# Summing sixteen states per channel block: from turned products of 128x128 to plain products of 128x512, with a different order of the prologue and of the work between the scans

## What is computed

```python
x_and_res = x @ W_in.T
xp, res = jnp.split(x_and_res, 2, axis=-1)
xc = silu(depthwise_conv(xp, conv_w, taps=4) + conv_b)
ssm = xc @ W_x.T                       # B, C of 16 states each, and one dt
dt = softplus(dt @ W_dt.T + b_dt)
A = -exp(A_log)
def step(h, inp):                      # over the tokens
    h = exp(A * dt_t) * h + dt_t * B_t * xt
    y_t = einsum('bed,bd->be', h, C_t) + D * xt
y = silu(y + res)
return y @ W_out.T
...
x = layernorm(x + mamba(x))
x = layernorm(x + moe_top2_of_8(x))
```

## Time and profile before

| | us |
|---|---|
| time, median of 3 runs | 1610.7 (1607.85 to 1612.19) |
| time of the profiled execution | 1612.57 |
| its span, first to last instruction | 1611.0 |
| first scan of block 0 | 61.5 |
| end of the last scan of block 7 | 995.7 |

### The profile page before, as it was taken

How to read it: one execution, slowest core, us unless ns; L and a number is a source line. 1 busy time by engine, 2 the same in 40 slices (tenths; PEclk the granted TensorE clock), 3 DMA queues, 4 the chain that set the end, 5 groups by cost and what they waited for, 6 DMA issues and landing times. The chain is left out here.

```text
span 1611.0 us, 29240 instructions
## 1 busy us (share of the span) xinstructions
PE 1336.9 (83%) x8770; PEld 1118.7 (69%) x8771; DVE 1157.4 (72%) x2036; ACT 1041.1 (65%) x1438; POOL 1059.9 (66%) x989
## 2 busy tenths in 40 slices
PE   3598898898798898798887796639999999999970
PEld 1367577576577576576577685439999999999970
DVE  2678888888888888888888687436666666666646
ACT  3798996996996996996996874413333333333334
POOL 0288878778877978877978888344444444444436
PEclk8699899999999899999899798659999999999995
DMA  2032132222222222222212223441343631511108
GB/s 98 14 99 80 63 105 76 76 80 89 92 77 89 85 84 89 92 78 88 89 67 85 90 85 122 131 129 53 107 133 117 199 121 39 160 39 40 33 26 308
DMA packets 85677, 150.12 MB, mean 93 GB/s; under 512 B 11408, under 2 KB 34576, under 8 KB 85584
## 3 DMA queue, kind: packets, MB, share of 16 engines
q1 hardware_dynamic: 70480, 116.91, 22.7%
q0 software_dynamic: 9888, 27.29, 5.1%
q10 hardware_dynamic: 5216, 4.74, 0.9%
HBM read 104.45 MB, written 44.45 MB: 92 GB/s over the span
## 5 line engine op out<-in xcount | busy, mean ns | idle before, releaser
L1019 POOL TENSOR_TENSOR arena<-arena 128x1024 f32<-128x1024 f32 x256 | 611.2, 2394 | 73.0 <-DVE arena L796 61.9
L397 PEld LDWEIGHTS d_ps<-ident,arena 128*128 128x128 f32 x2048 | 257.4, 150 | 203.0 <-DVE arena L796 101.5
L397 PE MATMUL d_ps<-ident,arena 128*128 128x128 f32 x2048 | 337.7, 291 | 73.0 <-DVE arena L796 67.5
L618 ACT ACTIVATE arena<-u_tok,b_tok 128x512 f32<-128x512 f32 x512 | 327.3, 713 | 74.4 <-PE d_ps L397 72.8
L796 DVE TENSOR_TENSOR_SCAN arena<-arena,carry,d_ps 128x512 f32<-128x512 f32 x256 | 320.6, 1271 | 74.2 <-PE d_ps L397 72.9
L796 DVE TENSOR_TENSOR_SCAN arena<-arena,d_ps 128x512 f32<-128x512 f32 x256 | 305.1, 1211 | 79.4 <-PE d_ps L397 67.6
L410 PE MATMUL y_ps<-ident,arena 128*128 128x128 f32 x2048 | 311.0, 282 | 40.6 <-POOL arena L1019 40.6
L410 PEld LDWEIGHTS y_ps<-ident,arena 128*128 128x128 f32 x2048 | 248.7, 147 | 47.3 <-POOL arena L1019 47.3
L1306 ACT ACTIVATE h_t<-ht_ps 128x512 f32<-128x512 f32 x142 | 84.5, 595 | 289.8 <-PE ht_ps L1361 289.8
L629 ACT ACTIVATE arena<-dt,neg_a 128x2048 f32<-128x2048 f32 x128 | 255.4, 1995 | 1.9 <-DVE arena L796 1.3
L1371 PEld LDWEIGHTS y_ps<-arena,h_parts 128*128 128x128 f32 x1704 | 214.4, 192 | 8.8 <-issue 4.0
(11 more groups left out here) (170 smaller groups left out, 1681.9 us busy)
## 6 DMA issues: line engine op xcount, KB each, us to landing
arena<-c_rows SPq DMA_DIRECT2D x128, 256.0 KB, 3.4
weight_parts<-arena SPq DMA_DIRECT2D x80, 256.0 KB, 3.8
arena<-weight_parts SPq DMA_DIRECT2D x20, 1024.0 KB, 5.3
arena<-in_pieces SPq DMA_DIRECT2D x80, 128.0 KB, 3.6
xg<-expert_rows POOLq DMA_DIRECT2D x71, 130.0 KB, 2.4
arena<-expert_out SPq DMA_DIRECT2D x16, 512.0 KB, 10.4
arena<-in_pieces SPq DMA_DIRECT2D x12, 512.0 KB, 7.2
x_t<-in_x_t SPq DMA_DIRECT2D x8, 512.0 KB, 5.5
```

What stands on the lines that cost most here:

```text
L397: last = nc.tensor.matmul(d_ps[:, c % 2, j * P:(j + 1) * P], ub[:, g % U_RING, j, c * P:(c + 1) * P], t.ident[:], start=True, stop=True, i ...
L618: nc.scalar.activation(ub[:, g % U_RING, j, :], u_tok[:, j, :], ACT.Identity, scale=b_tok[:, b % 2, j, n:n + 1]).then_inc(scaled, 1)
L1019: nc.gpsimd.tensor_tensor(h[:, g % H_RING, lo:hi, :], h[:, g % H_RING, lo:hi, :], c_row[:, g % C_RING:g % C_RING + 1, :].broadcast_to([P, ...
```

## The change

- `sum_states` keeps channels on the partitions: per step four matmuls with the identity as weights and 128x512 of states streaming, no transposes. `y_ps` now holds [channel, group, token].
- So `turn_y` and `yt_out` fall away; the gated output `ys` goes straight into the output projection. The silu of the sums is two instructions of 128x4x256. The gate takes `w_in` as weights and `x_t` as stream; the skip is 4 matmuls of 128x512 in place of 16 of 128x128.
- `ys` and the inputs `u` share one buffer, as `y_u` did before; `tmp` is gone.
- `D_RING` is 4 and decays are made three steps ahead, scaled inputs still two.
- The output projection, gates, ranks, skips, residuals, softplus sum, inputs and the router's steps stand at other quarters. `onehot` is one instruction in place of eight. Each row store of the router has a step of its own.
- Pieces per block fall from 10 to 8: the last expert's 16 pieces are split in the prologue, in the tiles of h (`first_part` on ACT, `first_rest` on POOL, loads and stores on SP); the first scan waits for their stores.
- The prologue has its own order on ACT: a second copy of the spread dt (`z2`) lets DVE make the linear part (`first_sizes`), the first scaled inputs are read from PSUM, and the decays of steps 0 to 2 are made before the loop. `w_in` comes in two loads, `x_t` on ACT's queue.
- In i = 8 the own weights are rounded at steps 3 to 10 in place of 6 to 13.

```diff
-D_RING = 3
+D_RING = 4
+DECAY_LEAD = 3
...
                 def sum_states(b, k):
-                    n, q = divmod(k, 4)
-                    g, half = STATE * b + n, q // 2
-                    pe.wait_ge(hc_done, 2 * g + half + 1)
+                    n, c = divmod(k, 4)
+                    g = STATE * b + n
+                    pe.wait_ge(hc_done, 2 * g + c // 2 + 1)
                     if k == 0 and b > 0:
-                        pe.wait_ge(ys_done, b)
-                    for j in (2 * (q % 2), 2 * (q % 2) + 1):
-                        for c in (2 * half, 2 * half + 1):
-                            last = nc.tensor.matmul(y_ps[:, j, c * P:(c + 1) * P],
-                                                    h[:, g % H_RING, c, j * P:(j + 1) * P], t.ident[:],
-                                                    start=(n == 0 and c == 0), stop=(n == STATE - 1 and c == EC - 1),
-                                                    is_transpose=True)
-                    if q == 3:
+                        pe.wait_ge(ys_done, 2 * b)
+                    last = nc.tensor.matmul(y_ps[:, c, :], t.ident[:], h[:, g % H_RING, c, :],
+                                            start=(n == 0), stop=(n == STATE - 1))
+                    if c == 3:
                         last.then_inc(sum_done, 1)
...
-        PIECE_STEPS = (0, 1, 3, 4, 6, 8, 9, 10, 11, 12)
-        PARTED = (EXPERTS - W_RING) * PIECES
+        PIECE_STEPS = (0, 1, 3, 4, 6, 8, 10, 12)
+        PARTED = (EXPERTS - W_RING - 1) * PIECES
...
                     act.wait_ge(sum_done, STATE * (r + 1))
-                    nc.scalar.activation(y_u[:], y_ps[:], ACT.Silu).then_inc(ys_done, 1)
+                    if r >= 1:
+                        wait_filled(act, "out1", r - 1)
+                    for lo in (0, T // 2):
+                        nc.scalar.activation(ys[:, :, lo:lo + T // 2], y_ps[:, :, lo:lo + T // 2], ACT.Silu)\
+                            .then_inc(ys_done, 1)
...
+                if i == -1:
+                    silu()
+                    act.wait_ge(t.rest_loaded, 16 * REST_LOADS)
+                    first_part(3)
+                    ssm_out()
+                    for c in range(EC):
+                        z_parts(c)
+                    soft_tail()
+                    nc.scalar.activation(t.neg_a[:], t.neg_a[:], ACT.Exp).then_inc(exp_done, 1)
+                    decays(0)
+                    xp_out(0)
+                    xp_out(1)
+                    wait_freed(act, "btok", 0)
+                    for j in range(TT):
+                        first_scale(j)
+                    for j in range(TT):
+                        ut_out(j)
+                    for j in range(TT):
+                        wait_freed(act, f"ut{j}", 0)
+                    scale(1)
+                    decays(1)
+                    decays(2)
+                    xp_out(2)
+                    xp_out(3)
+                    return
...
-                        if n == 7:
+                        if n == 8:
                             soft_tail()
...
                     if 0 <= g + LEAD < STEPS:
                         scale(g + LEAD)
-                        decays(g + LEAD)
+                    if 0 <= g + DECAY_LEAD < STEPS:
+                        decays(g + DECAY_LEAD)
...
                         if back:
-                            if at == (9, 1):
+                            if at == (7, 0):
                                 residual(0)
-                            if at == (11, 1):
+                            if at == (10, 0):
                                 residual(1)
```

More of the change, by code:

```diff
@@ L82, in _ @@
         def _(act):
+            for dst, src in early:
+                act.dma_start(dst, src).then_inc(t.first_loaded, 16)
             for dst, src in taps:
@@ L556, in between @@
+                        if 0 <= m < 8 and n < 7:
+                            out_projection(0, m, m + 1)
                     if front and at == (5, 0):
                         spread_z()
+                        if f == 0:
+                            spread_z2()
+                    if place and at == (7, 0):
+                        ranks()
+                    if front and at == (8, 1):
+                        turn_b()
                     if scans:
-                        gates = ((4, 2), (4, 3), (5, 1), (5, 2), (5, 3), (6, 0), (6, 2), (6, 3))
+                        gates = ((4, 0), (4, 3), (5, 2), (6, 1), (6, 3), (7, 1), (7, 2), (7, 3))
@@ L619, in scale, with first_scale @@
                                          scale=b_tok[:, b % 2, j, n:n + 1]).then_inc(scaled, 1)
+            def first_scale(j):
+                wait_filled(act, f"ut{j}", 0)
+                nc.scalar.activation(ub[:, 0, j, :], bank(f"ut{j}", 0), ACT.Identity,
+                                     scale=b_tok[:, 0, j, 0:1]).then_inc(scaled, 1)
             def decays(g):
@@ L753, in step @@
                         turned_out(1)
-                    if back and n == 3:
-                        yt_out(0)
-                    if back and n == 4:
-                        yt_out(1)
+                    if place and n == 4:
+                        router_exp()
                     if front and n in (5, 6):
@@ L760, in step @@
                         z_parts(2 * n - 9)
-                    if back and n in (5, 6):
-                        yt_out(n - 3)
-                    if place and n == 5:
-                        router_exp()
                     if front and n == 9:
@@ L768, in step @@
                         xp_out(n - 11)
+                    if back and n == 11:
+                        normed()
                     if front and n == 13:
@@ L771, in step @@
                         ut_out(1)
-                    if back and n == 14:
-                        normed()
                     if early and n == 15:
@@ L1117, in step @@
                         times_c(g - 1, 1)
+                    if place and n == 7:
+                        router_den()
+                    if place and n == 8:
+                        router_spread()
+                    if place and n == 9:
+                        router_weigh()
                     if scans:
```

229 lines of the change are left out of this document (129 added, 100 removed).

## The result

The changed kernel takes 1649.1 us (median of 4 runs, 1648.1 to 1650.8) against 1610.0 (1607.9 to 1612.2) before on the same chip: ratio 1.0244, 95% interval 1.0226 to 1.0262. It is slower by 39 us where 66 were forecast. The sign, the stretches that grew and the price of a sum came as written; what the other stretches lose between their engines was put too high, so that the time lies nearer to the rivals B (1639) and C (1645) than to 1677. The trace says where: the prologue gives 8.5 us (first scan at 53.0, before 61.5), the tail 6.2, and the scan phase takes 52.9 more (987.1 against 934.2).

What follows compares the result with a forecast made beforehand. PE was taken to set steps 4 to 8, 14 and 15. Scan phase +78 us, prologue -5, tail -7: +66 on the profiled 1612.6 gives 1678.6, as a median 1677; range 1635 to 1710, some 0.85.

Steps and rivals of the forecast that it cites:

- B: Whole kernel: interlocks are free, light steps take only what the fuller engine has, a block 125.0 us; 1639 us, chance 0.15.
- C: PE's clock: denser work keeps it at 2.4 GHz, worth -32 us; 1645 us in all, chance 0.10.
- PE sets steps 4 to 8, 14 and 15: Block 4: PE's work sets these steps; 4 to 8 grow by 9.8 us to 43.1, 14 and 15 by 3.4 to 16.4.
- rival E: Steps 4 to 8: ACT, equally full, sets them and not PE; 1544 us in all, chance 0.08.
- A sum costs 0.86 us: Sums on PE: a quarter's matmul takes 0.86 us where four transposes took 0.44, +27 us per block before savings.
- Steps 9 to 13: Block 4: steps 9 to 11 fall from 29.6 to 27.4 us, 12 and 13 grow from 13.13 to 14.3.
- Steps 0 to 3: Block 4: few sums, less ACT copying and a decay one step earlier; 28.5 us against 30.5, -2.0.
- Prologue: Before the scans: first scan at about 53 us instead of 61.51, counted as -5 us at step 1 (0 to -9).
- Tail: After the last sums: 8.5 us of turning and copying go, own weights take some back; -7 us (-3 to -9).
- A: Whole kernel: the main forecast, PE's longer sums set the full steps; 1677 us, chance 0.55.
- D: Blocks: each loses 8.5 us beyond the fuller engine, as before, and takes 134; 1710 us in all, chance 0.10.
- F: Whole kernel: the gains happen to meet the growth; 1611 us, chance 0.02.

Runs made afterwards that it cites:

- half-width sums: The changed kernel with 14 of the 16 states' sums over 256 of the 512 tokens, output not the reference's; 1577.9 us, ratio 0.979 to the kernel before.
- half decays: The kernel before with decays of two of the four channel groups left out after the first three steps, output not the reference's; 1597.9 us, ratio 0.992.
- b_both: The kernel before with half of the decays left out after the first three steps and a block's last sums one or two quarters later; 1591.1 us, ratio 0.987.
- h_late_ranks: The changed kernel's prologue and pieces, old turned sums, later places, router's ranks at step 7's third quarter instead of first; 1565.7 us, ratio 0.971 to the kernel before.

## Why the prediction was right, and where its size was off

**PE sets steps 4 to 8, 14 and 15: right, shown.** Forecast for steps 4 to 8 of block 4 were 8.21, 9.50, 8.21, 9.84 and 7.3 us; measured 8.20, 9.84, 8.19, 9.69 and 7.46, 43.4 against 43.1. Over blocks 2 to 6 they grew by 49.6 us, forecast +49. Step 5 is longer by the spreading of z: its two instructions of 1x512 start 1.05 us ahead of the next row, and their neighbours are 0.16 late, where 0.86 was put for all. Steps 14 and 15: 16.4 forecast, 16.40 measured. The half-width sums confirm the price, 0.43 us less for half the width; they and the half decays show that ACT was not the bound, which ends rival E.

**A sum costs 0.86 us: right.** The row of the gate's shape was the right one to take. The four transposes of a quarter cost half of it, 0.44 us in the earlier trace rows. The Trainium skill (TensorE: Matmul & The Clock Gate, Terms) has the transpose mode four times faster for FP32; these traces show a factor of two.

**Steps 9 to 13: right in kind, too high.** Steps 9 to 11 take 27.1 us in block 4 against 27.4, but this nearness is in part luck. PE's work was put at 25.0 there and 2.4 added, since "two engines that full cannot interlock without loss". PE stands for nothing in these three, and the 27.1 hold some 2 us of work of step 12: at the scan that begins step 12 eight transposes of that step are done, at the starts of steps 9 to 11 four. Steps 12 and 13 then take 13.3 us and not 14.3, with PE busy for 12.07. For the five steps together PE is busy for 39.2 us, against 38.9 of forecast work, and the loss beside it is 1.2 us where 2.8 was put. In the five blocks 9 to 11 fell from 149.8 to 131.6, -18 where -11 was forecast, since blocks 3 and 5 fell from 31.3 and 31.4 us to 26.5 and block 6 takes only 24.4; 12 and 13 stayed at 66.5 and 66.8, where +6 was forecast.

**Steps 0 to 3: the term that was mis-sized most.** Forecast 28.5 us for block 4, measured 25.2; in the five blocks -23 and not -10, which is 13 of the 24 us that were too much. I had counted what their own instructions lose and had left the rest as loss between four engines. But in steps 0 to 2 that loss came from products and inputs that were late on POOL and ACT (`b_both`). That the others catch up where one engine binds the stretch ahead is how I read it; no run shows it by itself.

**Block 6: a slip.** I took five alike. Block 6 has no `early` projections: its steps 12 to 15 had to grow less, and it takes 119.4 us against 119.8, where the four others take 126.2 against 120.4 on the mean. That is some 6 us of the 24 by which blocks 2 to 6 were put too high (+47 forecast, +22.7 measured); 3.4 of them lie in its steps 14 and 15, and 2.7 in 9 to 11.

**Blocks 0, 1 and 7**: +12.0, +9.6 and +8.6 against 11, 9 and 11. **Prologue**: first scan at 53.0 as forecast; of the 8.5 us gained I had let 3.5 go again at step 1, and 0.8 went, at step 0. Four early loads and stores held nothing up. **Tail**: -6.2 against -7.

**The rivals.** B (interlocks free, 1639) and C (the clock stays high, 1645) are what the measured 1649 lies next to. Block 4 takes 125.3 us, and 125.0 was B's sum for it; only the shares differ, with 25.2 and 27.1 for steps 0 to 3 and 9 to 11 where B had 26.0 and 25.2. So in these blocks B is nearer than A. C came together with it: PEclk over blocks 2 to 6 went from 0.95 to 0.98, over the program from 0.912 to 0.945 (just below the 0.95 that I had asked for). It rose in steps 9 to 15, from 0.94 to 1.00 in block 4. In steps 0 to 3 only block 4 went from 0.83 to 1.00; blocks 2, 3, 5 and 6 have 0.93, 0.93, 0.82 and 0.93 now and had 0.94, 0.89, 0.95 and 0.86. No run parts B from C. The half-width sums, with plain matmuls, fell to 0.75 in the step in which PE had stood for 2.8 us, and the turned sums of `h_late_ranks`, mostly transposes, hold 1.00 in steps 7 and 8 of block 4. What went ahead of a fall was idle time of PE, with either kind. The Trainium skill (TensorE: Matmul & The Clock Gate, Part 4) has transposes not counting as PE's activity; these traces don't need it and don't refute it, since no step of theirs holds transposes alone. D (blocks lose 8.5 us beyond the fuller engine, as before) fell: block 4 loses 0.3 beyond B's sum. F (1611) lies far below the measured interval.

**What would show it**: sums 0.86 apart, step 5 at 9.84 (9.5 was asked for), step 7 at 9.69 with PE never idle, DVE's wait at 136, step 11 at 9.8 without the wait for the residual, ACT idle 25.2 us in block 4, first scan at 53.0. Only PEclk of the whole missed its mark.

## What to carry to other kernels

Price an edit on the engine that sets each stretch, by the nearest row of the same shape: that sum held to 1% here over steps 4 to 8, and over 14 and 15. Don't carry the idle time of the other stretches over as a constant; follow from where their operands are late. And where two engines are nearly full, taking one wait away moves the loss to the next place that needs the other's queue: three such places (turned y, projection, ranks) had to be moved in turn before `h_late_ranks` kept the gain.

## What the runs showed of the hardware

In the scans of these traces PE's granted clock fell behind idle time of PE, and the price is then more than the idle time: in step 7 of the half-width sums PE stood for 2.8 us, and 6.8 us then ran at 1.2 GHz, the lower of the two levels (PEclk 0.50), though PE was busy for nearly all of them:

```profile
561.57:568.40 6.83, 6.22 (x21) 4.91 (x22) 1.25 (x2) 6.81 (x8) 3.65 (x7) 0.50 0.30 97
```

But the same idle time didn't always bring a fall. In step 1 of the changed kernel PE stands for 1.7 us in blocks 2, 4 and 6, with the same instructions around it; in block 4 the clock stayed at 1.00 through step 2, in blocks 2 and 6 3.4 us at 1.2 GHz followed, and in the kernel before it stayed at 1.00 behind a stand of 3.1 us (block 5, at 651 us). The changed kernel's block 2 at the fall, and step 2 of its block 4:

```profile
314.47:317.88 3.41, 3.41 (x10) 1.42 (x10) 2.44 (x4) 3.39 (x6) 3.33 (x3) 0.50 0.57 188
562.27:567.53 5.26, 4.66 (x34) 3.59 (x34) 4.56 (x5) 5.25 (x7) 5.10 (x6) 1.00 0.20 46
```

Short instructions on DVE can take as long as a product on POOL. In step 3 of `b_both` the eight `onehot` of 128x8 took 5.22 us in all, two of them 2.12 and 2.39 and the others 0.22 each; the two begin with or within POOL's products and end with them. DVE, then POOL:

```profile
533.08 5.22 DVE L876 TENSOR_SCALAR onehot<-iota_ef,ek 128x8 f32<-128x8 f32 x8
```

```profile
532.82 2.36 POOL L1020 TENSOR_TENSOR arena<-arena 128x1024 f32<-128x1024 f32 x1
...
535.39 2.36 POOL L1020 TENSOR_TENSOR arena<-arena 128x1024 f32<-128x1024 f32 x1
```

The second softplus sum of the earlier trace rows, 2.42 us where the first took 1.20, is of the same kind. The Trainium skill (GPSIMD Engine Reference, Specifications) has the SBUF interfaces shared by the two engines, with contention for DVE's instructions in a two-port mode or with two SBUF inputs; the row agrees for the softplus sum, which has two such inputs. The scans, which read the transposes from PSUM, keep their 1.21 us beside the products. In the kernel before it was not the `onehot` but a cast of 128x4 just ahead of it that was held so, for 1.15, 1.34 and 2.26 us in blocks 4 to 6, where such a cast takes 0.17 by itself.
